# Layer 1 of a four-layer network on one core: sums of the recurrence moved from TensorE to DMA transfers, z's transform as whole fp32 products

## The reference

```python
ek = jnp.exp(jnp.minimum(kf, 30.0))
ekv = ek * vf
...
num = nf + nb - ekv + euk * vf      # nf, nb: scans of ekv forward and backward
den = df + db - ek + euk            # df, db: scans of ek; euk = exp(min(u + k, 30))
base = jax.nn.sigmoid(r) * (num / jnp.maximum(den, 1e-08))
```

## Time and profile before

| | |
|---|---|
| three timed runs | 1756.54, 1758.97, 1759.94 us; median 1758.97 |
| the profiled execution | 1757.67 us, its span 1755.7 us |
| busy in the span | PE 1529.4 (87%), DVE 1135.0 (65%), ACT 990.8 (56%), POOL 334.5 (19%) |
| layer 1 | from 552.96 us (first instruction of its block) to 827.8 us |

### The profile page before, as it was taken

How to read it: one execution, slowest core, us unless ns; L and a number is a source line. 1 busy time by engine, 2 the same in 40 slices (tenths; PEclk the granted TensorE clock), 3 DMA queues, 4 the chain that set the end, 5 groups by cost and what they waited for, 6 DMA issues and landing times.

```text
span 1755.7 us, 20006 instructions
## 1 busy us (share of the span) xinstructions
PE 1529.4 (87%) x6574; PEld 989.4 (56%) x6574; DVE 1135.0 (65%) x1806; ACT 990.8 (56%) x1314; POOL 334.5 (19%) x251
## 2 busy tenths in 40 slices
PE   5666578899985999997559999789999999999997
PEld 2222234444443666664524444378888888888886
DVE  7899589899996999996828787945322222222222
ACT  6765588889994989996327787834311211211210
POOL 0000011111210000000524242552221331331311
PEclk9999798899997999999869999989999999999999
DMA  7764632312102543331965454581000100100001
GB/s 278 270 227 163 235 126 82 102 60 73 60 31 74 180 150 102 109 127 41 387 229 167 147 183 141 170 278 43 12 27 34 36 3 34 37 3 34 1 23 74
DMA packets 100808, 199.82 MB, mean 114 GB/s; under 512 B 11492, under 2 KB 28388, under 8 KB 96996
## 3 DMA queue, kind: packets, MB, share of 16 engines
q1 hardware_dynamic: 95012, 180.72, 30.3%
q0 software_dynamic: 5120, 16.78, 2.8%
q10 hardware_dynamic: 576, 1.05, 0.2%
HBM read 139.79 MB, written 58.72 MB: 113 GB/s over the span
## 4 chain that ended last, share of the span: by engine, by line
PE 45%; POOL 2%; DVE 2%; issue 2%; DMA 1%; ACT 1%; SPq 0%; DVEq 0%; POOLq 0%; ACTq 0%
PE ffn_po L2506 10%; PE ffn_pg L2487 10%; PE ffn_pu L2487 10%; PE moe_psum L1918 7%; PE moe_psum L1939 3%; PE ffn_po L1613 2%; POOL tokens_by_slot L2123 1%; PE ffn_po L1600 1%; PE moe_psum L1906 1%; DVE x L2576 1%; DMA in_part<-expert_out,moe_source 0%; PE moe_psum L1929 0%; DVE x L1646 0%; PE moe_psum L1874 0%; DMA moe_zr<-ratio 0%
## 5 line engine op out<-in xcount | busy, mean ns | idle before, releaser
L2409 ACT ACTIVATE up_front<-ffn_pg,ffn_gate_chunk 128x512 f32<-128x512 f32 x64 | 44.1, 689 | 320.7 <-PE ffn_pg L2487 271.7
L2566 DVE SCALAR_TENSOR_TENSOR up_front<-ffn_pu,ffn_up_scale,up_front 128x512 f32<-128x512 f32 x64 | 48.1, 751 | 231.5 <-PE ffn_pu L2487 231.5
L2576 DVE SCALAR_TENSOR_TENSOR x<-ffn_po,ffn_out_scale,x 128x512 f32<-128x512 f32 x128 | 87.2, 745 | 148.1 <-PE ffn_po L2506 148.1
L2460 POOL TENSOR_TENSOR ffn_hl<-up_front,ffn_hh 128x512 fp32r<-128x512 f32 x64 | 82.7, 1294 | 396.6 <-ACT ffn_hh L2416 396.5
L961 POOL TENSOR_TENSOR l_rr<-l_rr,constants 128x1 f32<-128x1 f32 x32 | 28.8, 901 | 483.6 <-DVE l_rr L988 483.6
L2506 PE MATMUL ffn_po<-ffn_hh,ffn_wh 128*128 128x512 f32 x256 | 101.3, 396 | 4.2 <-DVE x L2576 2.9
L2487 PE MATMUL ffn_pg<-zhi,ffn_wh 128*128 128x512 f32 x256 | 101.5, 396 | 0.5
L2487 PE MATMUL ffn_pu<-zhi,ffn_wh 128*128 128x512 f32 x256 | 100.8, 394 | 0.0
L2506 PE MATMUL ffn_po<-ffn_hh,ffn_wl 128*128 128x512 f32 x256 | 100.6, 393 | 0.0
L2487 PE MATMUL ffn_pg<-zhi,ffn_wl 128*128 128x512 f32 x256 | 100.4, 392 | 0.0
L2487 PE MATMUL ffn_pu<-zhi,ffn_wl 128*128 128x512 f32 x256 | 100.4, 392 | 0.0
(11 more groups left out here) (351 smaller groups left out, 4098.1 us busy)
## 6 DMA issues: line engine op xcount, KB each, us to landing
wkv_k<-in_fside SPq DMA_DIRECT2D x64, 256.0 KB, 4.0
ratio<-wkv_fn SPq DMA_DIRECT2D x64, 256.0 KB, 2.3
wkv_ek<-exp_k SPq DMA_DIRECT2D x48, 256.0 KB, 3.1
wkv_ekv<-exp_k_times_v SPq DMA_DIRECT2D x48, 256.0 KB, 4.0
moe_zt<-tokens_by_slot SPq DMA_DIRECT2D x39, 256.0 KB, 2.9
expert_out<-moe_eo SPq DMA_DIRECT2D x39, 256.0 KB, 2.0
up_front<-in_gated SPq DMA_DIRECT2D x8, 1024.0 KB, 5.0
x<-in_x SPq DMA_DIRECT2D x4, 1024.0 KB, 8.0
```

Of the source, the lines that this page charges most:

```text
L2409: eng.activation(hf[t], p_g[t][:, :], ACT.Silu, scale=scale).then_inc(*E(f"silu{t}").inc)
L2460: eng.tensor_tensor(hl[t][slot % 2][:, :], hf[t], hh[t][slot % 2][:, :].bitcast(F32), ALU.subtract).then_inc(*E(f"hl{t}").inc)
L2566: eng.scalar_tensor_tensor(hf[t], p_u[t][:, :], scale, hf[t], ALU.mult, ALU.mult).then_inc(*E(f"h{t}").inc)
L2576: last = eng.scalar_tensor_tensor(x[:, o, :], p_o[:, o, :], out_s[:, o:o + 1], x[:, o, :], ALU.mult, ALU.add)
```

## The change

In `layer1` and in `Wkv` (other layers keep their form):

1. **bd is added to fd, bn to fn, and k to fn by DMA transfers** that GpSimd issues (`accum_op=ALU.add`, 128x512 fp32 each, both sides in SBUF): `add_later_d`, `add_later_n`, `add_now_n`. `den_on_tensor` multiplies two parts (eu, fd), and waits for the transfer; `num_on_tensor` and `take_num` are gone, and `quotient` reads fn.
2. **z is multiplied whole in fp32**; `split_z` and `low_z` are gone.
3. **The down weights' chunks are multiplied whole in fp32** (`WholeTransform`, one fp32 product in place of two fp32r ones); `high` and `low` are gone. The stream runs two steps later.
4. **The order within the steps is new on every engine.** `scan_d` and `scan_n` work one step earlier (lag 0 in place of 1), `newton` and `recip_exp` one step earlier (lag 1 in place of 2), the load of k (`load_values`) is apart from the loads of ek and ekv and one step later in SyncE's list.

```diff
-class DownTransform:
...
-    def high(self, eng, i, p):
-        eng.wait_ge(*self.loaded[p].at(i // 2))
-        if i >= 2:
-            eng.wait_ge(*self.E("product").at(i - 2))
-            eng.wait_ge(*self.E("lo").at(i - 2))
-        eng.activation(self.hi[p][:, :], self.a[p], ACT.Copy).then_inc(*self.E("hi").inc)
-
-    def low(self, eng, i, p):
-        eng.wait_ge(*self.E("hi").at(i))
-        eng.tensor_tensor(self.lo[p][:, :], self.a[p], self.hi[p][:, :].bitcast(F32), ALU.subtract).then_inc(*self.E("lo").inc)
...
+        self.added = {n: core.queue_event(self.tag + n + "_added", slots) for n in added}
...
+    def done(self, name, i):
+
+        if name in self.added:
+            return self.added[name][i % self.slots].at(i // self.slots)
+        return self.E(name).at(i)
+
     def load(self, eng, i, p):
+        self.load_values(eng, i, p)
+        self.load_exps(eng, i, p)
+
+    def load_values(self, eng, i, p):
         if i >= self.slots:
-            eng.wait_ge(*self.E("num").at(i - self.slots))
+            eng.wait_ge(*self.done("num", i - self.slots))
         eng.dma_start(self.k[p][:, :], self.d["fside"][:, ds(i * TIME, TIME)]).then_inc(*self.k_in[p].inc)
+
+    def load_exps(self, eng, i, p):
...
         bank = self.banks[0]
         eng.wait_ge(*self.E("exps").at(i))
         eng.wait_ge(*self.E("ends").at(min(i, self.slots - 1)))
-        eng.wait_ge(*self.E("scan_d").at(i))
+        eng.wait_ge(*(self.done("both", i) if "both" in self.added else self.E("scan_d").at(i)))
         if i >= 1:
-            eng.wait_ge(*self.E("num_out" if len(self.banks) == 1 else "den_out").at(i - 1))
-        for t, part in enumerate((self.eu, self.fd, self.bd)):
-            last = eng.matmul(bank[:, :], self.c["ident"][:, :], part[p][:, :], start=t == 0, stop=t == 2)
+            eng.wait_ge(*self.E("num_out" if len(self.banks) == 1 and "num" not in self.added else "den_out").at(i - 1))
+        parts = (self.eu, self.fd) if "both" in self.added else (self.eu, self.fd, self.bd)
+        for t, part in enumerate(parts):
+            last = eng.matmul(bank[:, :], self.c["ident"][:, :], part[p][:, :], start=t == 0, stop=part is parts[-1])
         last.then_inc(*self.E("den").inc)
...
+    def add_later_d(self, eng, i, p):
+        eng.wait_ge(*self.E("scan_d").at(i))
+        eng.wait_ge(*self.E("ends").at(min(i, self.slots - 1)))
+        eng.dma_start(self.fd[p][:, :], self.bd[p][:, :], accum_op=ALU.add).then_inc(*self.added["both"][p].inc)
+
+    def add_later_n(self, eng, i, p):
+        eng.wait_ge(*self.E("scan_n").at(i))
+        eng.wait_ge(*self.E("ends").at(min(i, self.slots - 1)))
+        eng.dma_start(self.fn[p][:, :], self.bn[p][:, :], accum_op=ALU.add).then_inc(*self.added["later"][p].inc)
+
+    def add_now_n(self, eng, i, p):
+        eng.wait_ge(*self.done("later", i))
+        eng.wait_ge(*self.E("euv").at(i))
+        eng.dma_start(self.fn[p][:, :], self.k[p][:, :], accum_op=ALU.add).then_inc(*self.added["num"][p].inc)
...
-        rt, gate, zh, zl = pair("rt", CH), pair("gate", CH), pair("zh", CH, F32R), pair("zl", CH, F32R)
+        rt, gate = pair("rt", CH), pair("gate", CH)
...
-        dt = DownTransform(core, s, lambda i: every16(down_mid)[:, ds(i * CH, CH)],
-                           lambda i: every16(down_full)[:, ds(i * CH, CH)], H16, p_h, "down_second")
-        w = Wkv(core, s, c, d, wkv_out, 2, 2, preloads=("recip",), banks=[core.banks(s, "l1_wkv", [P, TIME])])
+        dt = WholeTransform(core, s, lambda i: every16(down_mid)[:, ds(i * CH, CH)],
+                            lambda i: every16(down_full)[:, ds(i * CH, CH)], H16, p_h, "down_second")
+        w = Wkv(core, s, c, d, wkv_out, 2, 2, preloads=("recip",), added=("both", "later", "num"),
+                banks=[core.banks(s, "l1_wkv", [P, TIME])])
...
-            for j in range(TILES + 3):
+            for j in range(TILES + 4):
                 for i in due(j, 0, TILES):
                     load(i, i % 2)
                 for i in due(j, 0, TILES):
-                    w.load(eng, i, i % w.slots)
-                for i in due(j, 0, TILES):
+                    w.load_exps(eng, i, i % w.slots)
+                for i in due(j, 1, TILES):
+                    w.load_values(eng, i, i % w.slots)
+                for i in due(j, 3, TILES):
+                    w.store(eng, i, i % w.slots)
+                for i in due(j, 2, TILES):
                     dt.load(eng, i, i % 2)
-                for i in due(j, 3, TILES):
+                for i in due(j, 4, TILES):
                     dt.store(eng, i, i % 2)
                 for m in due(j, 2, UP_AHEAD):
                     load_up(eng, m)
-                for i in due(j, 2, TILES):
-                    w.store(eng, i, i % w.slots)
...
             def hadamard_z(i, p):
                 eng.wait_ge(*H_built.at(H_last))
-                eng.wait_ge(*h16_ready.at(0))
-                eng.wait_ge(*E("zl").at(i))
+                eng.wait_ge(*E("z").at(i))
                 if i >= 1:
                     eng.wait_ge(*E("qt1").at(i - 1))
                 for k in range(CT):
-                    for t, part in enumerate((zh, zl)):
-                        last = eng.matmul(p_z[:, :], part[p][:, k * P:(k + 1) * P],
-                                          hadamard_row(k),
-                                          start=(k + t == 0), stop=(k == CT - 1 and t == 1))
+                    last = eng.matmul(p_z[:, :], z[p][:, k * P:(k + 1) * P], hadamard_row(k).bitcast(F32),
+                                      start=k == 0, stop=k == CT - 1)
...
+            eng.wait_ge(*h16_in.at(0))
             for j in range(TILES + 4):
                 for i in due(j, 1, TILES):
+                    hadamard_z(i, i % 2)
+                for i in due(j, 1, TILES):
+                    w.den_on_tensor(eng, i, i % w.slots)
+                for i in due(j, 3, TILES):
                     dt.product(eng, i, i % 2)
-                for i in due(j, 1, TILES):
-                    hadamard_z(i, i % 2)
                 for i in due(j, 3, TILES):
                     cols_of_q2(i, i % 2)
-                for i in due(j, 1, TILES):
-                    w.den_on_tensor(eng, i, i % w.slots)
                 for i in due(j, 4, TILES):
                     cols_of_y(i, i % 2)
                 for i in due(j, 2, TILES):
@@ -1274,20 +1254,11 @@
                     hadamard_h1(i, i % 2)
                 for i in due(j, 1, TILES):
                     up(i, i % 2)
-                for i in due(j, 1, TILES):
-                    w.num_on_tensor(eng, i, i % w.slots)
...
-            def split_z(i, p):
-                eng.wait_ge(*E("z").at(i))
-                if i >= 2:
-                    eng.wait_ge(*E("rows_of_z").at(i - 2))
-                    eng.wait_ge(*E("zl").at(i - 2))
-                eng.activation(zh[p][:, :], z[p][:, :], ACT.Copy).then_inc(*E("zh").inc)
...
                     y_out(i, i % 2)
-                for i in due(j, 2, TILES):
-                    w.recip_exp(eng, i, i % w.slots)
                 for i in due(j, 0, TILES):
                     gate_row(i, i % 2)
                 for i in due(j, 1, TILES):
                     round1(i, i % 2)
-                for i in due(j, 0, TILES):
-                    dt.high(eng, i, i % 2)
                 for i in due(j, 3, TILES):
                     q2_cols(i, i % 2)
+                for i in due(j, 3, TILES):
+                    dt.evacuate(eng, i, i % 2)
                 for i in due(j, 1, TILES):
                     q1_cols(i, i % 2)
                 for i in due(j, 1, TILES):
                     w.take_den(eng, i, i % w.slots)
-                for i in due(j, 0, TILES):
-                    split_z(i, i % 2)
                 for i in due(j, 1, TILES):
                     w.ln(eng, i, i % w.slots)
                 for i in due(j, 1, TILES):
-                    dt.evacuate(eng, i, i % 2)
+                    w.recip_exp(eng, i, i % w.slots)
                 for i in due(j, 1, TILES):
                     relu_h(i, i % 2)
                 for i in due(j, 1, TILES):
                     square_h(i, i % 2)
                 for i in due(j, 2, TILES):
                     round2(i, i % 2)
-                for i in due(j, 1, TILES):
-                    w.take_num(eng, i, i % w.slots)
+
+        @block.gpsimd
+        def _(eng):
+            for j in range(TILES + 2):
+                for i in due(j, 2, TILES):
+                    w.add_later_n(eng, i, i % w.slots)
+                for i in due(j, 2, TILES):
+                    w.add_now_n(eng, i, i % w.slots)
+                for i in due(j, 1, TILES):
+                    w.add_later_d(eng, i, i % w.slots)
...
             for j in range(TILES + 4):
-                for i in due(j, 1, TILES):
-                    w.scan_d(eng, i, i % w.slots)
                 for i in due(j, 2, TILES):
-                    sums_and_differences(i, i % 2)
+                    sums_of_h(i, i % 2)
```

(26 more changed lines are left out.)

70 lines of the change are left out of this document (18 added, 52 removed).

## The result

The changed kernel takes 1746.59 us (median of 4 runs, 1745.37 to 1747.82), the kernel before, on the same chip, 1759.18 (4 runs). The ratio is 0.9935, with a 95% interval of 0.9922 to 0.9948: 12.6 us less; 1738 us was predicted. The profiled execution is that of 1747.82 us, span 1746.0.

A forecast was written before the change was run, and what follows sets the result against it. TensorE, busy throughout layer 1's even stretch, was taken as the bound: its step goes 15.96 - 5.98 + 4.30 = 14.28 us. Thirteen steps x 1.68 = 21.8, less 0.9 at the end, take 1758.97 to 1738 us, own range 1734 to 1743.

The forecast's parts named there:

- rival 2: Layer 1's transfers late, but not by all of the gain: steps of 14.3 to 15.8 us, 1739 to 1757; chance 0.11.
- rival 1: Layer 1's engines wait for each other in turn, VectorE keeping its 0.64 us wait: step 14.75 us, 1744; chance 0.15.
- g and L: GpSimd's accumulating transfers in layer 1: g for issuing, 1.25 us, L for landing, 5.8 us; together 7.05, range 4.9 to 10.7.
- the sign under which the prediction was to fall: For layer 1's additions: the prediction falls if an accumulating transfer costs over twice a gather.
- The 2.95 us issue: Warning in the earlier trace: a GpSimd issue took 2.95 us, not 0.95, beside a two-operand VectorE instruction; one makes g + L 7.65.
- The loop's formula: Layer 1, from products over the sum to max2: loop takes g + L + 6.3 us, costing more than today's step over 9.7.
- Rival 3: Accumulating transfers decide layer 1's step at den_on_tensor: g + L 10.7, loop 17.0 us, 14 us more, 1773; chance 0.16.
- I take zero: Layer 1's start: z's saved split against a first denominator waiting for cap's cleared column; no net change, 2 us either way.

The follow-up runs named there:

- the sums back on TensorE: Changed kernel with the numerator and the denominator's third part back on TensorE, take_num back on ScalarE, no accumulating transfer; ratio 1.0160 to the kernel before.
- z whole alone: Kernel before with only z multiplied as whole fp32 products, without its split, no accumulating transfer; ratio 1.0145 to the kernel before.
- all three holdups gone: Changed kernel with 1 MB loads in steps 16 to 19, denominator's addition first in GpSimd's list, columns cleared early; about 10 us less than the changed kernel.
- the extra load waited for: Changed kernel with one more 256 KB load each step, issued and waited for by GpSimd ahead of the denominator's addition; ratio 1.0110 to the kernel before.

## Why the prediction was right, and by how much it was off

The way was right, and the main mechanism: TensorE was the bound, and its work fell. The size was not: 12.6 us in place of 20.9. The measured 1746.6 lies above the forecast's own range (1734 to 1743) and in that of rival 2 (1739 to 1757), which had a chance of 0.11. That rival 1's number, 1744, is the nearest is luck; its mechanism is absent.

**The step.** Forecast 14.28, measured 14.42. z cost 3.43 against 3.44, the down chunk 0.86 as priced. The 0.14 lies in up and down: 3.52 now, 1.80 + 1.54 = 3.34 before. Two runs place it. With the sums back on TensorE, down takes 1.73 until the whole fp32 product of z behind it starts (696.48 to 698.21); with z whole alone, where an fp32r product stands behind down, it takes 1.54 as before (696.01 to 697.55). Why wasn't tried. VectorE's work was forecast at 14.11 and is 14.09; ScalarE's at 12.8, and is 13.2 (14.42 less its one wait of 1.21 for the sums). So rival 1, engines waiting in turn, did not come: VectorE's wait fell from 0.64 at `max1` to 0.33 at `max2`, and TensorE never waits in a full step.

**g and L.** Forecast 1.25 + 5.8 = 7.05; measured 1.09 + 6.0 = 7.1 in the step shown, and 1.09 + 5.3 = 6.4 with the median of ten. The share too: 32.7% of 140 us over 29 transfers is 1.58 us of all 16 engines for each, against the 1.54 assumed from twice a plain one; at 2.05 times a plain one (1.58/0.77) the cost stood just over the sign under which the prediction was to fall, and did no harm in the full steps. The 2.95 us issue had no counterpart: the addition of k at 706.06 was issued beside the whole of `gated`, two operands in SBUF, and took 0.85, as did the one at 710.81 beside small instructions. That agrees with the Trainium skill, page SBUF — State Buffer, section "Who interferes with whom", which infers that such an instruction doesn't hold the making of descriptors. The estimate from the Trainium skill, page DMA: Bandwidth & Descriptors, section "Anatomy of one DMA", 2.6 us for 256 KB, is under every median landing of an addition here (3.9 to 6.3); the measurements decide.

**The loop's formula was wrong, its threshold nearly right.** It was written as step >= g + L + 6.3, as if the next `products` came at a fixed time. But `products` itself stands behind `max2`, by the rest of VectorE's list (12.9 us, 707.04 to 719.94). From one `products` over the sum, the denominator and `max2` to the next `products` but one lie two steps, so twice the step >= g + L + 7.66 + 12.9. At a step of 14.42 the one forgives g + L up to 8.1 and the other up to 8.3; but a delay beyond it costs half as much a step, so the point at which the change would lose was 11.4 (2 x 15.96 - 20.56), not 9.7. Rival 3, with g + L of 10.7, would by that have been a step of 15.6, no loss. By this formula the chance of slower was put too high.

**The step that failed is the start, "I take zero", 2 us either way.** The forecast counted thirteen steps at the new pace; two of them lie ahead of the fifth sum and one behind the fifteenth. Part by part, in us against the kernel before:

```
                            forecast        measured, first profile   all three holdups gone
up to the third sum          0                +3.1                      -1.1
the next two steps          -3.4              +0.4                      -3.1
ten full steps             -16.8             -15.4                     -15.4
the rest                    -1.7 + 0.9        +0.7                      -0.6
layer 1                    -20.9             -11.1                     -20.3
```

Of the 9.8 us that are missing, 6.9 are late additions in the start and in two steps that were counted as full ones, 1.4 are the 0.14 a step, and 1.5 the end. In the second profile of the same kernel, at a granted clock of 1.00 throughout the end, the rest was 0.6 less than in the kernel before, near the forecast's 0.8. L was taken as one number for the layer from a quiet part of it, while the start is where four 1 MB loads run; the DMA share there was in the earlier trace rows, 0.49 against 0.39, and went unread. What I named for the start, the column that `cap` clears, was real (3 us) but is one of three. What happened is rival 2, transfers partly late, in four steps of sixteen, not in all. With the three holdups gone the layer is 254.18 us, and the forecast holds part by part.

## What to carry to other kernels

When work goes from an engine to a transfer, its landing time becomes part of a dependency: look at every stretch for what else is on the DMA engines at that moment, and move large loads that nobody needs soon out of it. In a queue of transfers on one engine, the one that is awaited first goes first, and no wait for another transfer stands ahead of it. Find how many steps a loop of waits spans before pricing a delay: over two steps it costs half.

## What the runs showed of the hardware

- An addition of 256 KB inside SBUF lands in 3.9 us (median) when it is the first of a pair, and in 5.0 to 5.4 when another was issued 0.55 to 0.8 us before it, whichever of the two it is. The one from bn, issued 4 to 5 us behind the second of a pair, takes 5.2 to 5.5. In the first steps, beside 1 MB loads, one into fd took 10.5 and one into fn 11.3.
- GpSimd's issue of one takes 0.85 to 1.52 us in the records, but the next can begin 0.55 us after the first.
- The length of TensorE's wait alone doesn't tell the granted clock of its step (1.00 is 2.4 GHz, 0.50 would be 1.2). With the extra load waited for, steps with waits of 2.61, 3.52 and 2.90 us had 0.91 in the mean, but the two with 2.38 and 2.86 us, one directly behind the other, had 1.00. In the changed kernel the steps with 1.84 and 1.31 us had 1.00, and in its second profile the one with 2.64 us had 0.91. Each undisturbed step behind one at 0.91 was back at 1.00.
- Over the same work at the end of the layer the granted clock was 1.00 in one profile of the changed kernel and as low as 0.73 in the other, at a price of 1.3 us.
